# Attention on one core: projections and V spread over the steps, denominators and V in the output's PSUM bank

## The chip, the core and the metric

The kernel runs on one core of a Trainium2 chip. The metric is the device time of one execution in microseconds; the runs of the kernel before took 3674.70, 3674.92 and 3675.24 us (median 3674.92). Five engines share the work, each with a queue of its own that runs in order: TensorE (PE; its weight loads are shown as PEld), VectorE (DVE), ScalarE (ACT), GpSimd (POOL) and SyncE (SP, which issues DMAs). They wait for one another by semaphores.

## The reference, cut to what matters

The program chains four blocks (attention with feed-forward, a residual convolution block, whitening, a state-space block). The change touches attention alone:

```python
x_ln = layer_norm(x_flat, g1, beta1)               # 16 images, 1024 positions, 64 channels
q, k, v = jnp.split(x_ln @ w_qkv.T, 3, axis=-1)    # 8 heads of 32
scores = jnp.einsum('bhqd,bhkd->bhqk', q, k) * HEAD_DIM ** (-0.5)
attn = jax.nn.softmax(scores, axis=-1)
out = jnp.einsum('bhqk,bhkd->bhqd', attn, v)
```

## The kernel before, in words

Layer normalisation has written `scratch_xn`. `attention_phase` (from L144) takes 16 images of 8 heads, in groups of 4 heads (the 128 partitions): 32 groups, one *period* each. A period has 16 steps: 2 halves of 512 queries by 8 blocks of 128 keys (`s`, and `half, kb = divmod(s, 8)`). A lead-in period comes first; the stages are called lead, first, mid and last. Each engine's block has a `period` of its own, an order written out by hand, and the orders meet in counted semaphores.

In a step TensorE makes the scores of 4 heads, transposed (keys on partitions), in fp32 (L398), and adds the negated row maxima to them with a matmul over one row of ones (L402) from `nrow`. ScalarE takes two heads at a time through exp into `probs` (L479). The scores fill one set of four PSUM banks, so a pair of the next step waits until that pair has been read. TensorE then adds the product of V and `probs` of an earlier step into the bank `O` (`values`, L410).

Beside this, for the next group, TensorE makes bf16 scores in the other orientation (`maxima`, L334): four matmuls a step into a ring of three PSUM banks, which VectorE reduces to maxima (L526). After the eight quads of a half VectorE combines them (L534), TensorE turns them (`turn`, L372) and ScalarE copies them to `nrow`. `LATE` says by how many steps the maxima of a group run into its own period. The ring also takes all else: the projections q and k for the next group (`project`, L347), copied by ScalarE to `QT`, `KT` (L461) and cast by VectorE from the same bank to bf16 `QH`, `KH` (L542); V's projection in two banks (`values_projected`, L360); the denominators (`denominators`, L385). `extra` names the step in which each of these stands, and `wait_for_bank` makes TensorE wait until a bank's last reader is done.

A denominator is the sum of `probs` over all keys. GpSimd adds blocks 0 to 5 of a half (L580, five additions into `prob_sums`); a matmul with ones then sums blocks 6 and 7 and `prob_sums`, one step after the half has ended. ScalarE makes exp(-ln) of it (L461, L465), VectorE multiplies `O` by that into `att` (`normalise`, L549), and only then may TensorE start the next half's values in `O`. SP stores `att` and loads the next image's `xn` (L286, L282).

Of the kernel before, what the change touches and what calls it, by code (L numbers as in the profile page):

```python
# [11 lines left out]
P = 128  # L12
# [135 lines left out]
def attention_phase(nc, sem, xn_d, wqkvT, ident_bf, attn_d):  # L148
# [3 lines left out]
    LATE = 3  # L152
# [12 lines left out]
    def executed(stage, kind, which, s):  # L165

        ahead = kind in MADE_AHEAD or (kind == "turn" and which == 0) or (kind == "max" and s >= LATE)
        if stage == "lead":
            return ahead
        if stage == "last":  # L170
            return not ahead
        return not (stage == "first" and kind == "den" and which == 1)
# [45 lines left out]
    with ExitStack() as ctx:  # L218
# [25 lines left out]
                 "negm_done", "sc_ready", "exp_done", "pv_done", "pool_sums", "lden_done", "rden_done", "od_free")  # L244
        (consts_in, consts_set, xn_in, max_ready, max_done, extra_ready, extra_done, cast_done, negm_done, sc_ready,
         exp_done, pv_done, pool_sums, lden_done, rden_done, od_free) = (sem(f"at_{n}") for n in names)
# [12 lines left out]
        def first_groups(grp):  # L259
            return isinstance(grp, int) and grp <= 0  # L260

        def casts(grp, kind, which):
            return 4 * (grp + 1) + 2 * which + "qk".index(kind) + 1
# [11 lines left out]
        def _(sp):  # L275
# [13 lines left out]
            def image(b, stage):  # L289
                if stage != "first":  # L290
                    store(b - 1, 1, 1)
                if stage != "last":

                    at = "first" if stage == "first" else "mid"
                    sp.wait_ge(extra_ready, unit_count(at, GROUPS * b, unit_of(at, "v", 1)))
# [16 lines left out]
        def _(pe):  # L312
# [3 lines left out]
            def wait_for_bank(stage, grp, unit):  # L316
                before = same_bank_before(stage, grp, unit)
                if before:
                    pe.wait_ge(max_done if before[2][1] == "max" else extra_done, unit_count(*before))
                    if before[2][1] in "qk":  # L320

                        pe.wait_ge(cast_done, casts(before[1], *before[2][1:3]))

            def maxima(stage, grp, par, s, heads):
# [4 lines left out]
                if quad == 0 and heads[0] == 0:  # L329
                    pe.wait_ge(cast_done, 4 * (grp + later) + 4)  # L330
# [6 lines left out]
            def project(stage, grp, par, half):  # L337
                if not executed(stage, "q", half, 0):
                    return
                if half == 0 and par == 1:  # L340
                    pe.wait_ge(xn_in, (grp + 3) * DMA)
                units = [unit_of(stage, kind, half) for kind in "qk"]
                for n, unit in enumerate(units):
                    wait_for_bank(stage, grp, unit)
                    rows = slice(n * C, (n + 1) * C)
                    at = n * INNER + (1 - par) * P
                    nc.tensor.matmul(ring[:, unit[3], :], w[rows, at:at + P], xn[rows, hs(half)],  # L347
                                     start=True, stop=True).then_inc(extra_ready, 1)

            def values_projected(stage, grp, par):  # L350
                if not executed(stage, "v", 0, 6):
                    return
                units = [unit_of(stage, "v", n) for n in range(2)]
                for unit in units:
                    wait_for_bank(stage, grp, unit)
                at = 2 * INNER + (1 - par) * P
                for k in range(KB):
                    n = k % 2
                    rows = slice(n * C, (n + 1) * C)
                    m = nc.tensor.matmul(ring[:, units[n][3], blk(k // 2)], xn[rows, blk(k)], w[rows, at:at + P],  # L360
                                         start=True, stop=True)
                    if k >= KB - 2:
                        m.then_inc(extra_ready, 1)
# [12 lines left out]
            def denominators(stage, grp, half):  # L376
                if not executed(stage, "den", half, 0):
                    return
                unit = unit_of(stage, "den", half)
                wait_for_bank(stage, grp, unit)  # L380
                pe.wait_ge(pool_sums, SUMMED * (2 * (grp - half) + half + 1))
                srcs = [probs[:, k, :, :] for k in range(SUMMED + 1, KB)] + [prob_sums[:, half, :, :]]
                for n, src in enumerate(srcs):
                    for h in range(GH):
                        m = nc.tensor.matmul(ring[head(h), unit[3], :], ones[:, head(h)], src[:, h, :],  # L385
                                             start=(n == 0), stop=(n == len(srcs) - 1))
                m.then_inc(extra_ready, 1)

            def scores(stage, grp, par, s):
                half, kb = divmod(s, KB)  # L390
                if kb == 0:

                    at = stage if half else stage_before(stage, grp)
                    pe.wait_ge(extra_done, unit_count(at, grp if half else grp - 1, unit_of(at, "turn", half)))
# [10 lines left out]
            def values(grp, par, s):  # L405
                half, kb = divmod(s, KB)
                if kb == 0 and not (isinstance(grp, int) and grp == 0 and half == 0):
                    pe.wait_ge(od_free, 2 * grp + half)
# [4 lines left out]

            def period(grp, par, stage):
                for s in range(STEPS):
                    if stage != "lead":
                        scores(stage, grp, par, s)
                    maxima(stage, grp, par, s, (0, 1))
                    if s < 2:
                        project(stage, grp, par, s)  # L420
                    if s % KB == 1 and stage != "lead":
                        denominators(stage, grp, 1 - s // KB)
                    if s == 4 or s == 12:
                        turn(stage, grp, 1 if s == 4 else 0)
                    if s == 6:
                        values_projected(stage, grp, par)
                    if stage != "lead":
                        if s == 0:
                            if stage != "first":
                                values(grp - 1, 1 - par, STEPS - 1)  # L430
                        elif s % KB == 2:
                            values(grp, par, s - 2)
                            values(grp, par, s - 1)
                        elif s % KB != 1:
                            values(grp, par, s - 1)
                    maxima(stage, grp, par, s, (2, 3))
                if stage == "last":
                    pe.wait_ge(exp_done, 2 * STEPS * NG)
                    values(grp, par, STEPS - 1)
                    D = ring[:, 0, :]  # L440
                    pe.wait_ge(max_done, counted_before(N_MAX, grp) + N_MAX["last"])
                    pe.wait_ge(extra_done, counted_before(N_EXTRA, grp) + N_EXTRA["last"])
                    pe.wait_ge(pool_sums, SUMMED * 2 * NG)
# [1297 lines left out]
```

## Time and profile before

| | us |
|---|---|
| median of three runs | 3674.92 |
| profiled execution, span | 3666.4 |
| of it, first to last exponential of attention | about 1869 |
| TensorE busy (its matmuls overlap) | 3163.0 |
| VectorE busy | 2573.4 |
| GpSimd busy | 2214.4 |
| ScalarE busy | 2006.1 |

The span is that of one profiled execution, from its first to its last instruction; some 8.5 us of the measured time lie around it. Times below are us from the start of the span. A timeline row gives the start, the time from first start to last end, the engine, the line and operation, the tiles (out<-in), the shapes and the number of instructions merged; in brackets stands the idle time before it and what ended it. In fp32 one matmul of the program is two records. Records of matmuls on different rows or columns of the array overlap, so TensorE's pace is read from starts, not from busy time.

### The profile page before, as it was taken

The numbers are of one execution on the slowest core, as the hardware profiler recorded it, in microseconds if no ns is written. First come the engines' busy times: TensorE is split into PE (matmuls) and PEld (weight loads), VectorE is DVE, ScalarE is ACT, GpSimd is POOL, SyncE is SP. The second block draws the span as 40 slices with busy tenths as digits, with TensorE's granted clock in tenths as the row PEclk, the third lists the DMA queues.
The fourth block names the chain that finished last, engine by engine and source line by source line (L and its number), as shares of the span: only waits on it lengthen the run. The fifth ranks groups of instructions, "written<-read, shape, count | busy, mean of one in ns | idle before, by whom it ended". The sixth has DMA issues, their size and how long they took to land. (4 is left out here: it accounts for less than half of the span.)

```text
span 3666.4 us, 55668 instructions
## 1 busy us (share of the span) xinstructions
PE 3163.0 (86%) x18550; PEld 1183.9 (32%) x18550; DVE 2573.4 (70%) x3346; ACT 2006.1 (55%) x2381; POOL 2214.4 (60%) x684
## 2 busy tenths in 40 slices
PE   6999999999999999999995899774888888887787
PEld 2333333333333333333331233341322222222222
DVE  5777777777767777777771222142888988988988
ACT  3566666666656666666663333223555564565554
POOL 0577777777777777777776000003657666666666
PEclk7899999999999999999998999886989999999999
DMA  2000000000000000000003211114333433443443
GB/s 103 12 16 10 16 16 16 16 13 16 16 17 10 16 16 16 19 10 16 16 10 74 92 69 46 48 64 149 119 132 128 155 142 120 153 150 118 147 150 115
DMA packets 74739, 234.86 MB, mean 64 GB/s; under 512 B 13088, under 2 KB 14180, under 8 KB 74420
## 3 DMA queue, kind: packets, MB, share of 16 engines
q1 hardware_dynamic: 69460, 215.06, 17.3%
q0 software_dynamic: 5056, 16.83, 1.3%
q8 instruction: 139, 2.28, 0.3%
q14 instruction: 84, 0.69, 0.1%
HBM read 192.42 MB, written 39.39 MB: 63 GB/s over the span
## 5 line engine op out<-in xcount | busy, mean ns | idle before, releaser
L526 DVE TENSOR_REDUCE at_pmax<-at_ring 128x1 f32<-128x512 f32 x2048 | 1300.8, 685 | 392.0 <-PE at_ring L334 381.2
L479 ACT ACTIVATE at_probs<-at_sc 128x1024 f32<-128x1024 f32 x1024 | 992.5, 1021 | 531.7 <-PE at_sc L402 529.7
L580 POOL TENSOR_TENSOR at_prob_sums<-at_prob_sums,at_probs 128x2048 f32<-128x2048 f32 x256 | 1159.0, 4527 | 74.8 <-ACT at_probs L479 54.5
L398 PE MATMUL at_sc<-at_QT,at_KT 32*128 32x512 f32 x4096 | 782.5, 634 | 4.1 <-issue 3.7
L1634 POOL TENSOR_TENSOR ss_drive<-ss_du,ss_bsb 128x1024 f32<-128x1024 f32 x261 | 610.7, 2352 | 263.9 <-DVE ss_state L1591 257.1
L1534 ACT ACTIVATE ss_decay<-ss_delta,ss_a 128x512 f32<-128x512 f32 x520 | 354.5, 687 | 447.6 <-DVE ss_state L1587 299.5
L410 PE MATMUL at_O<-at_probs,at_V 128*32 128x512 f32 x4096 | 535.3, 606 | 52.5 <-DVE at_att L549 51.6
L580 POOL TENSOR_TENSOR at_prob_sums<-at_probs 128x2048 f32<-128x2048 f32 x64 | 290.7, 4543 | 403.1 <-ACT at_probs L479 403.1
L1423 PE MATMUL ss_Y<-ss_seen,ss_ident 128*128 128x512 f32 x1032 | 520.7, 628 | 0.0
L334 PE MATMUL at_ring<-at_KH,at_QH 32*128 32x512 bf16 x2048 | 442.3, 387 | 5.7 <-DVE at_pmax L526 2.9
L1599 DVE TENSOR_TENSOR ss_seen<-ss_state,ss_C 128x1024 f32<-128x1024 f32 x259 | 316.3, 1221 | 80.4 <-PE ss_C L1411 72.6
L1591 DVE TENSOR_TENSOR_SCAN ss_state<-ss_decay,ss_state,ss_drive 128x512 f32<-128x512 f32 x259 | 332.3, 1283 | 33.6
L1587 DVE TENSOR_TENSOR_SCAN ss_state<-ss_decay,ss_drive 128x512 f32<-128x512 f32 x259 | 314.9, 1216 | 32.0 <-POOL ss_drive L1634 16.2
L334 PEld LDWEIGHTS at_ring<-at_KH,at_QH 32*128 32x128 bf16 x2048 | 149.6, 92 | 554.5 <-DVE at_pmax L526 345.0
L1411 PE MATMUL ss_C<-ss_bc,ss_select 96*128 96x512 bf16 x518 | 161.0, 393 | 191.5 <-DVE ss_seen L1599 190.9
L402 PE MATMUL at_sc<-at_nrow,at_ones_bf 1*128 1x512 bf16 x2048 | 315.5, 379 | 0.0
L1423 PEld LDWEIGHTS ss_Y<-ss_seen,ss_ident 128*128 128x128 f32 x1032 | 202.3, 200 | 228.7 <-issue 175.5
L398 PEld LDWEIGHTS at_sc<-at_QT,at_KT 32*128 32x128 f32 x4096 | 256.3, 184 | 50.3 <-ACT at_probs L479 40.8
L938 POOL DMA_DIRECT2D scratch_x<-fc_out x8 | 4.3, 534 | 345.9 <-ACT fc_out L839 345.9
L410 PEld LDWEIGHTS at_O<-at_probs,at_V 128*32 128x32 f32 x4096 | 87.4, 108 | 249.3 <-issue 165.9
L1411 PEld LDWEIGHTS ss_C<-ss_bc,ss_select 96*128 96x128 bf16 x518 | 40.4, 101 | 385.8 <-DVE ss_seen L1599 322.7
L347 PE MATMUL at_ring<-at_xn,at_w 64*128 64x512 f32 x256 | 123.7, 679 | 26.6 <-DMA at_xn<-scratch_xn 19.3
(199 smaller groups left out, 2695.6 us busy)
## 6 DMA issues: line engine op xcount, KB each, us to landing
ss_bsb<-scratch_rows SPq DMA_DIRECT2D x265, 512.0 KB, 6.9
scratch_attn<-at_att SPq DMA_DIRECT2D x64, 256.0 KB, 2.0
fc_att<-scratch_attn SPq DMA_DIRECT2D x32, 512.0 KB, 5.8
ss_xn<-scratch_xm SPq DMA_DIRECT2D x34, 256.0 KB, 5.6
at_xn<-scratch_xn SPq DMA_DIRECT2D x32, 256.0 KB, 3.8
ss_xw<-scratch_xw SPq DMA_DIRECT2D x17, 256.0 KB, 3.9
ln_x<-in_x SPq DMA_DIRECT2D x8, 512.0 KB, 4.2
scratch_xn<-ln_xn POOLq DMA_DIRECT2D x8, 512.0 KB, 3.0
```

What stands on the lines that cost most here:

```text
L334: nc.tensor.matmul(ring[:, unit[3], :], QH[head(h), p, blk(quad // 2)], KH[head(h), p, hs(quad % 2)], start=True, stop=True).then_inc(max_ ...
L398: nc.tensor.matmul(sc[:, h, :], KT[head(h), par, blk(kb)], QT[head(h), par, hs(half)], start=True, stop=False)
L402: m = nc.tensor.matmul(sc[:, of, :], ones_bf[row, :], nrow[row, half, :], start=False, stop=True)
L410: m = nc.tensor.matmul(O[head(h), :], V[:, par, kb, head(h)], probs[:, kb, h, :], start=(kb == 0), stop=(kb == KB - 1))
L479: nc.scalar.activation(probs[:, kb, two, :].rearrange("p h q -> p (h q)"), sc[:, two, :].rearrange("p h q -> p (h q)"), ACT.Exp, scale=SCA ...
L526: nc.vector.tensor_reduce(pmax[:, quad // 2, h, quad % 2:quad % 2 + 1], ring[:, unit[3], :], AX_X, ALU.max, negate=True).then_inc(max_done, 1)
L580: nc.gpsimd.tensor_tensor(prob_sums[:, half, :, :], before, probs[:, k, :, :], ALU.add).then_inc(pool_sums, 1)
L1423: m = nc.tensor.matmul(Y[:, hs(h)], ident[:], seen[:, n % DEPTH, hs(h)], start=False, stop=(n == N - 1))
L1534: nc.scalar.activation(decay[:, hs(h)], delta[:, par, hs(h)], ACT.Exp, scale=a_neg[:, n:n + 1])\
L1591: nc.vector.tensor_tensor_scan(now[:, hs(1)], decay[:, hs(1)], drive[:, n % DEPTH, hs(1)], now[:, HALF - 1:HALF], ALU.mult, ALU.add).then_ ...
L1599: nc.vector.tensor_tensor(seen[:, n % DEPTH, :], state[:, n % 2, :], Cp[:], ALU.mult).then_inc(seen_done, 1)
L1634: nc.gpsimd.tensor_tensor(drive[:, n % DEPTH, :], du[:, par, :], bsb[:, n % SLOTS, :], ALU.mult).then_inc(drive_done, 1)
```

## The change

The plan of a period is drawn up anew; no arithmetic goes except two casts' source.

- Projections stand singly: q0 in step 0, k0 in 2, k1 in 3, q1 in 11 (before: q0 and k0 in step 0, q1 and k1 in step 1). Their casts read `QT` and `KT` in SBUF instead of the ring bank, and stand behind the step's reductions.
- V's projection leaves the ring. It is made in two halves, in steps 3 and 11, each of four key blocks in the bank `O`, and copied from there.
- Denominators leave the ring too. When the last values of a half are in `O` (step 0 or 8), ScalarE copies `O` unnormalised to `att`; then TensorE sums blocks 6 and 7 in `O` (step 1 or 9) and adds `prob_sums` (step 2 or 10), and ScalarE takes Ln from `O`. `normalise` multiplies `att` in place, one step later than before.
- `O` is thus used in turn by the values, the denominators and V, with a wait at each change of hands.
- Values are added two blocks at a time: none in steps 1 to 3 of a half, blocks 0 and 1 in its step 4, 2 and 3 in 5, 4 and 5 in 6, 6 in 7, and 7 in the next half's step 0.
- `LATE` goes from 3 to 5; the turns move to steps 7 and 15. The wait for a turn stands between the scores of heads 0 and 1 and their maxima's matmul, not ahead of all scores.

```diff
-    LATE = 3
+    LATE = 5
-    extra = {0: [("q", 0), ("k", 0)], 1: [("q", 1), ("k", 1), ("den", 1)], 4: [("turn", 1)], 6: [("v", 0), ("v", 1)],
-             9: [("den", 0)], 12: [("turn", 0)]}
-    MADE_AHEAD = ("q", "k", "v")
+    extra = {0: [("q", 0)], 2: [("k", 0)], 3: [("k", 1)], 7: [("turn", 1)], 11: [("q", 1)], 15: [("turn", 0)]}
+    MADE_AHEAD = ("q", "k")
+    DIRECT_AT, SUMS_AT, V_AT = 1, 2, 3
+
+    LAST_KB = KB - 1
+    PV_AT = {0: (LAST_KB,), 4: (0, 1), 5: (2, 3), 6: (4, 5), 7: (6,)}
...
                 if before:
                     pe.wait_ge(max_done if before[2][1] == "max" else extra_done, unit_count(*before))
-                    if before[2][1] in "qk":
-
-                        pe.wait_ge(cast_done, casts(before[1], *before[2][1:3]))
...
+            def values_projected(stage, grp, par, half):
+                if stage == "last":
                     return
+                if stage == "lead" or (stage == "first" and half == 0):
+                    if v_halves(grp, half) > 1:
+                        pe.wait_ge(v_done, v_halves(grp, half) - 1)
+                else:
+                    pe.wait_ge(lden_done, 2 * grp + half)
                 at = 2 * INNER + (1 - par) * P
+                rows = slice(half * C, (half + 1) * C)
+                for n in range(KB // 2):
+                    k = half * KB // 2 + n
+                    m = nc.tensor.matmul(O[:, blk(n)], xn[rows, blk(k)], w[rows, at:at + P], start=True, stop=True)
+                m.then_inc(v_ready, 1)
...
+            def denominator(src, start, stop):
+                for h in range(GH):
+                    m = nc.tensor.matmul(O[head(h), :], ones[:, head(h)], src[:, h, :], start=start, stop=stop)
+                return m
+
+            def denominators_direct(of_half):
+                pe.wait_ge(raw_done, of_half + 1)
+                for k in range(SUMMED + 1, KB):
+                    denominator(probs[:, k, :, :], k == SUMMED + 1, False)
+
+            def denominators_sums(of_half, half):
+                pe.wait_ge(pool_sums, SUMMED * (of_half + 1))
+                denominator(prob_sums[:, half, :, :], False, True).then_inc(den_ready, 1)
...
                     nc.tensor.matmul(sc[:, h, :], KT[head(h), par, blk(kb)], QT[head(h), par, hs(half)], start=True, stop=False)
+                    if kb == 0 and h == 1:
+                        at = stage if half else stage_before(stage, grp)
+                        pe.wait_ge(extra_done, unit_count(at, grp if half else grp - 1, unit_of(at, "turn", half)))
...
                     maxima(stage, grp, par, s, (0, 1))
+                    if closes and kb == DIRECT_AT:
+                        denominators_direct(2 * grp + half - 1)
+                    if closes and kb == SUMS_AT:
+                        denominators_sums(2 * grp + half - 1, was_half)
+                    if kb == V_AT:
+                        values_projected(stage, grp, par, half)
                     if stage != "lead":
+                        for k in PV_AT.get(kb, ()):
+                            if kb:
+                                values(stage, grp, par, half, k)
+                            elif closes:
+                                values(stage, was_grp, was_par, was_half, k)
+                    for kind, which in extra.get(s, []):
+                        if kind == "turn":
+                            turn(stage, grp, which)
+                        else:
+                            project(stage, grp, par, kind, which)
                     maxima(stage, grp, par, s, (2, 3))
...
+            def take_raw(grp, half):
+                act.wait_ge(pv_done, STEPS * grp + KB * (half + 1))
+                if not (isinstance(grp, int) and grp == 0):
+                    act.wait_ge(att_stored[half], grp * DMA)
+                nc.scalar.activation(att[:, half, :], O[:], ACT.Copy).then_inc(raw_done, 1)
...
+                nc.scalar.activation(lden[:], O[:], ACT.Ln).then_inc(lden_done, 1)
...
+            def take_v(grp, par, half):
+                act.wait_ge(v_ready, v_halves(grp, half))
+                nc.scalar.activation(V[:, 1 - par, half * KB // 2:(half + 1) * KB // 2, :].rearrange("p k d -> p (k d)"), O[:],
+                                     ACT.Copy).then_inc(v_done, 1)
...
-                    nc.vector.tensor_copy(to[:, 1 - par, hs(which)], ring[:, unit[3], :]).then_inc(cast_done, 1)
+                nc.vector.tensor_copy(to[:, 1 - par, hs(which)], of[:, 1 - par, hs(which)]).then_inc(cast_done, 1)
...
-                nc.vector.tensor_tensor(att[:, half, :], rden[:], O[:], ALU.mult).then_inc(od_free, 1)
+                nc.vector.tensor_tensor(att[:, half, :], att[:, half, :], rden[:], ALU.mult).then_inc(od_free, 1)
```

On ScalarE, `take_raw`, the two steps of the reciprocal, `take_v` and the copies of a step's `extra` stand in this order behind the two exponentials of their step.

## Rows read from the trace of the kernel before

**Rows 1.** Windows: us, then busy us of PE, PEld, DVE, ACT, POOL; clock, DMA.
```profile
1164.90:1223.10 58.20, 55.27 (x468) 21.05 (x465) 44.64 (x73) 37.59 (x45) 45.32 (x11) 1.00 0.06 19
104.90:1974.50 1869.60, 1770.76 (x14728) 669.45 (x14722) 1392.18 (x2246) 1197.55 (x1399) 1446.38 (x320) 0.99 0.05 14
54.50:104.90 50.40, 37.07 (x94) 9.66 (x94) 35.21 (x60) 5.25 (x8) 0.00 (x0) 0.50 0.08 19
```

**Rows 2.** Waits of the period from 1164.9 to 1223.1: total us, times, longest.
```profile
ACT at_probs L479 <- PE at_sc L402: 16.5, 15, 2.3
DVE at_pmax L526 <- PE at_ring L334: 11.6, 13, 2.1
```

**Rows 3.** Timeline of TensorE, steps 7 and 8 of that period.
```profile
1192.84 1.24 PE L398 MATMUL at_sc<-at_QT,at_KT 32*128 32x512 f32 x8
...
1194.03 0.38 PE L334 MATMUL at_ring<-at_KH,at_QH 32*128 32x512 bf16 x2
1194.34 1.06 PE L410 MATMUL at_O<-at_probs,at_V 128*32 128x512 f32 x8
...
1195.34 1.58 PE L398 MATMUL at_sc<-at_QT,at_KT 32*128 32x512 f32 x6
...
1197.49 1.06 PE L410 MATMUL at_O<-at_probs,at_V 128*32 128x512 f32 x8
...
1198.50 1.35 PE L398 MATMUL at_sc<-at_QT,at_KT 32*128 32x512 f32 x8
```

**Rows 4.** Timeline of TensorE, steps 0, 1, 4 and 6 of that period.
```profile
1165.66 2.01 PE L347 MATMUL at_ring<-at_xn,at_w 64*128 64x512 f32 x4
1167.60 1.06 PE L410 MATMUL at_O<-at_probs,at_V 128*32 128x512 f32 x8
...
1172.01 1.92 PE L385 MATMUL at_ring<-at_probs,at_ones 128*32 128x512 f32 x16
...
1174.73 0.39 PE L334 MATMUL at_ring<-at_KH,at_QH 32*128 32x512 bf16 x2
...
1183.63 0.40 PE L372 MATMUL at_ring<-at_ident,at_negm 128*128 128x128 bf16 x4
1183.96 1.06 PE L410 MATMUL at_O<-at_probs,at_V 128*32 128x512 f32 x8
...
1190.75 1.16 PE L360 MATMUL at_ring<-at_w,at_xn 64*128 64x128 f32 x16 [0.82 <-DVE at_pmax L526]
1191.84 1.07 PE L410 MATMUL at_O<-at_probs,at_V 128*32 128x512 f32 x8
```

**Rows 5.** Timeline of ScalarE in that period, with the next one's first exponentials.
```profile
1164.89 1.94 ACT L479 ACTIVATE at_probs<-at_sc 128x1024 f32<-128x1024 f32 x2 [0.56 <-PE at_sc L402]
...
1174.86 0.60 ACT L461 ACTIVATE at_lden<-at_ring 128x512 f32<-128x512 f32 x1 [1.96 <-PE at_ring L385]
...
1176.12 1.94 ACT L479 ACTIVATE at_probs<-at_sc 128x1024 f32<-128x1024 f32 x2
...
1194.23 1.94 ACT L479 ACTIVATE at_probs<-at_sc 128x1024 f32<-128x1024 f32 x2 [1.20 <-PE at_sc L402]
...
1223.07 1.94 ACT L479 ACTIVATE at_probs<-at_sc 128x1024 f32<-128x1024 f32 x2 [0.56 <-PE at_sc L402]
```

**Rows 6.** Groups of instructions, VectorE: shapes, count | busy us, mean ns.
```profile
L542 DVE CAST at_QH<-at_ring 128x512 bf16<-128x512 f32 x64 | 44.3, 692 | 54.1 <-ACT at_QT L461 54.1
...
L900 DVE COPY fc_pad<-fc_pad 64x512 f32<-64x512 f32 x32 | 12.1, 418 | 90.8 <-ACT fc_pad L823 90.8
```

**Rows 7.** The line of the state-space stage's scan: ns min/median/max.
```profile
L1587 DVE TENSOR_TENSOR_SCAN ss_state<-ss_decay,ss_drive x259: 1200/1217/1225, 2553.0 to 3654.9; 128x512 f32<-128x512 f32 x130
```

**Rows 8.** Timeline of the state-space stage: GpSimd's additions.
```profile
2960.49 13.89 POOL L1634 TENSOR_TENSOR ss_drive<-ss_du,ss_bsb 128x1024 f32<-128x1024 f32 x6 [0.25 <-POOL ss_du L1648]
```

**Rows 9.** Timeline of GpSimd in attention: a half's additions, the next half's first.
```profile
1148.37 18.34 POOL L580 TENSOR_TENSOR at_prob_sums<-at_prob_sums,at_probs 128x2048 f32<-128x2048 f32 x4
1172.00 4.54 POOL L580 TENSOR_TENSOR at_prob_sums<-at_probs 128x2048 f32<-128x2048 f32 x1 [5.29 <-ACT at_probs L479]
```

More of the change, by code:

```diff
@@ L169, in executed @@
             return ahead
-        if stage == "last":
-            return not ahead
-        return not (stage == "first" and kind == "den" and which == 1)
+        return not ahead if stage == "last" else True
     def period_units(stage):
@@ L328, in maxima @@
                 p = par if later == 0 else 1 - par
-                if quad == 0 and heads[0] == 0:
-                    pe.wait_ge(cast_done, 4 * (grp + later) + 4)
+                for kind, which, at in (("k", 0, 0), ("k", 1, 1), ("q", 1, KB)):
+                    if quad == at and heads[0] == 0:
+                        pe.wait_ge(cast_done, casts(grp + later - 1, kind, which))
                 for h in heads:
@@ L335, in maxima, with project @@
                                      start=True, stop=True).then_inc(max_ready, 1)
-            def project(stage, grp, par, half):
-                if not executed(stage, "q", half, 0):
+            def project(stage, grp, par, kind, half):
+                if not executed(stage, kind, half, 0):
                     return
-                if half == 0 and par == 1:
+                if (kind, half) == ("q", 0) and par == 1:
                     pe.wait_ge(xn_in, (grp + 3) * DMA)
[L342 to L348, printed above, removed]
@@ L350, in values_projected @@
-            def values_projected(stage, grp, par):
-                if not executed(stage, "v", 0, 6):
-                    return
-                units = [unit_of(stage, "v", n) for n in range(2)]
-                for unit in units:
-                    wait_for_bank(stage, grp, unit)
-                at = 2 * INNER + (1 - par) * P
[L357 to L363, printed above, removed]
+                unit = unit_of(stage, kind, half)
@@ L403, in scores, with values @@
                         m.then_inc(sc_ready, 1)
[L405 to L408, printed above, removed]
+            def values(stage, grp, par, half, kb):
+                if kb == 0:
+                    if stage == "last":
+                        pe.wait_ge(lden_done, 2 * grp + half)
+                    else:
+                        pe.wait_ge(v_done, v_halves(grp, half))
+                if kb == KB - 1:
+                    pe.wait_ge(exp_done, 2 * (STEPS * grp + KB * half + kb) + 2)
                 for h in range(GH):
@@ L412, in values, with half_before @@
                 m.then_inc(pv_done, 1)
+            def half_before(grp, par, half):
+                return (grp, par, 0) if half else (grp - 1, 1 - par, 1)
             def period(grp, par, stage):
                 for s in range(STEPS):
+                    half, kb = divmod(s, KB)
+                    closes = stage != "lead" and not (stage == "first" and half == 0)
+                    was_grp, was_par, was_half = half_before(grp, par, half)
                     if stage != "lead":
@@ L469, in period @@
                     half, kb = divmod(s, KB)
+                    closes = stage != "lead" and not (stage == "first" and half == 0)
                     if stage != "lead":
```

136 lines of the change are left out of this document (51 added, 85 removed).

## Prediction

> **What bounds the kernel now.** I read the stretches of the windows view first, then the waits of one period, then the PE and ACT timelines of that period. Attention has 32 periods of 16 steps, 1870 of the 3666.4 us between its first exponential and its last [rows 1], and nothing outside attention is touched. A regular period, from the first exponential of one group to that of the next, takes 1223.07 - 1164.89 = 58.18 us [rows 5]. In it VectorE is busy 44.6 us, ScalarE 37.6, GpSimd 45.3, and the granted clock is 1.00 (2.4 GHz) [rows 1]: no engine but TensorE is near full, and TensorE's 55 us count overlapping matmuls. ScalarE waits 16.5 us for scores and VectorE 11.6 us for maxima, both from TensorE [rows 2]. So the order of TensorE's queue, and the places where it stands still, set the period.
>
> A plain step shows the unit of work [rows 3]. Scores start at 1192.84 (call it T), the values matmul starts 1.50 us later and takes 1.00 us, and the next scores start at 1195.34: 2.50 us without a gap. The exponentials start at T + 1.39 and the pair ends at T + 3.33 (1194.23 and 1.94 long) [rows 5]. That is 0.83 us after the next scores began; the second pair of heads needs that half of the score banks, so in the next step the values matmul comes 1.32 us after the end of the exponentials (1197.49 against 1196.17) and the step takes 3.16 us. Hence my rule: the work behind the scores starts at T + 1.50 or at E + 1.32, whichever is later, E being the end of the exponentials of the step before. A step in which TensorE has about 0.8 us more to do covers ScalarE for nothing.
>
> **The ledger before.** TensorE's extra pieces, each measured to the start of the next piece [rows 4]: denominators of three sources 1174.73 - 1172.01 = 2.72, so 0.86 for each source after the first, which costs 1.00 as a values matmul does; a V projection 1.09; a turn 0.33; q and k one behind the other 1.94, about 1.0 each when not side by side. A period then holds 16 x 1.50 + 15.7 for the values (two of them in pairs at 1.86) + 5.4 + 2.1 for q and k side by side + 1.1 + 0.7 = 49 us. The other 9 us are waits: for ring banks around the doubled projections (steps 0, 1, 6), for the normalisation before the first values of a half (steps 2, 10), and for exponentials in the short steps (3, 4, 8, 12, 14).
>
> **The change, part by part.** *It adds work to TensorE.* Four single projections cost 4.0 instead of 2.1, and V in two halves 2 x 1.09 instead of 1.09. V's bound: a half uses one row half alone, with as many matmuls in series as now run in each of two streams; if the two streams gain nothing today it is 0.55, so 0.55 to 1.09, and I take 1.09 because the serial pace is what the row shows. Work per period goes from 49 to about 52.
>
> *It takes waits away.* The steps, by the rule above (values pairs 1.86, direct denominators 1.86, sums 1.00):
> - steps 4 to 6 and 12 to 14: 1.50 + 1.86 = 3.36 each. E falls at T + 3.33, just covered.
> - steps 7 and 15: 1.50 + 1.00 + 0.33, plus a little for the ring bank under the turn: 2.90.
> - steps 8 and 0: a new wait. The bias matmul now waits for the turned maxima of the step before, whose copy on ScalarE stands behind its exponentials: T7 + 3.33 + 0.60 = 1.03 us into step 8. Behind it in TensorE's queue stand the scores of heads 2 and 3, and behind them all else. 1.03 + 1.32 + 1.00 = 3.35; step 0 has q0 as well, 4.35.
> - steps 1 and 9: 1.50 + 1.86 = 3.36. The direct denominators wait for the copy of the output, done at about 0.7 us into the step (E plus 0.6) against the 1.50 at which they could start. Cover 0.8.
> - step 10: 1.50 + 1.00 = 2.50; step 2 with k0: 3.50.
> - step 11: E is 0.83 into it, so 2.15, then V and q1, 2.09: 4.24. V waits for the Ln that empties the bank, done 1.4 us into the step. Cover 0.8. Step 12's values wait for the copy of V, which ends about 0.3 us into step 12. Cover 1.2.
> - step 3: ScalarE has exponentials, Ln, Exp (1.26 us until the next exponential could start [rows 5]) and then the copy of k0 from the ring: 3.33 + 1.26 + 0.60 - 3.50 = 1.69 us into step 3. The first maximum behind it uses that ring bank and waits; its place was 1.2 [rows 3]. So 2.0 + 2.09 = 4.09.
>
> Sum: 4.35 + 3.36 + 3.50 + 4.09 + 10.08 + 2.90 = 28.28 for the first half and 3.35 + 3.36 + 2.50 + 4.24 + 10.08 + 2.90 = 26.43 for the second, 54.71 in all: 3.47 us less than 58.18, 6%.
>
> *What is moved on the other engines.* ScalarE gets two copies more (0.6 each), of V the same two: 38.8 us of 54.7. VectorE keeps its reductions; its casts now read SBUF. A cast from PSUM takes 692 ns; a copy of 64 x 512 fp32 between SBUF tiles took 418 [rows 6], so the casts cost between 0.42 and 0.69 and gain nothing on the path. The normalisation reads SBUF twice instead of SBUF and PSUM, 0.69 taken as it is; it comes one step later and TensorE no longer waits for it, and its store leaves one step later, with a period in hand. The loads of the next image move from step 6 to step 11 on SP's queue and have five steps, over 16 us, until step 0 needs them. GpSimd's five additions take 4.54 + 18.34 us [rows 9] and must be done by the sums of step 2 or 10: they start at E of step 1, so end 26.3 us later, some 6 us before they are asked for. With a half of 26.4 us they still fit.
>
> *Ends.* Two of thirteen maxima steps leave the lead-in, which runs at 0.50 of the clock [rows 1] and at VectorE's pace, 44.64 / 73 = 0.61 us each: 8 x 0.61 = 5 us. The last group gains about what a regular one does.
>
> Against the profiled execution: 3666.4 - 32 x 3.47 - 5 = 3550 us of span. The 8.5 us between the span and the median of 3674.92 stay: **3559 us**.
>
> **A rule of the Trainium skill against a row.** In the state-space stage a scan with two SBUF inputs takes 1200 to 1225 ns in all 259 cases [rows 7], while GpSimd's additions run one behind another, six in 13.89 us [rows 8]: neither slows the other. The Trainium skill, page "SBUF — State Buffer", section "Who interferes with whom", says that a VectorE instruction with two SBUF inputs contends with a GpSimd instruction that reads SBUF. By it the new normalisation could stand up to an addition's 4.5 us; by the rows it stands not at all, and the trace disagrees with the rule.
>
> **Rivals.**
> 1. *The casts stand behind GpSimd's additions* (the slower side). No row before shows a fast copy on VectorE beside a GpSimd addition, so its price lies between 0 and one addition, 4.53 us, for each cast. If a cast cannot start until the running addition ends, and VectorE's reductions queue behind it: with an addition every 4.58 us from 3.33 us into step 1, k0's cast is due 8.6 us after T1, inside the second addition (7.9 to 12.5). It waits 3.9 us; the maxima of step 3 find no bank, and the step grows by 3.4. k1's cast meets the next one and costs 1.1, q1's 0.2; q0's falls in GpSimd's idle time. 54.7 + 4.7 = 59.4 us, 1.2 more than now: 3674.9 + 38 - 5 = **3708 us**. It decides against the change as soon as the four casts together hold TensorE for more than 3.5 us in a period. For it: GpSimd is busy 45 of 58 us [rows 1]. Against it: the rows of the scans, which show no such thing for two-input operations. The same section of the Trainium skill says that casts between SBUF tiles may run in a two-port mode, and that the second of the two to issue then blocks fully; no run here shows it yet.
> 2. *The covers are too thin.* The output's bank changes hands between TensorE and ScalarE six times a period, with covers of 0.8 to 1.2 us. If half of these cost a copy of 0.6, the period is 56.5: 32 x 1.7 + 5 = 59 less, **3616 us**. For it: ScalarE takes its work in order, behind the exponentials.
> 3. *The change does nothing for the period*: what TensorE gains as waits it gives back as work (3 us more), **3675 us**. Against it: the waits before add to 9 us.
>
> **How the numbers follow.** Forecast 57%; rival 2 17%; rival 1 17%; rival 3 5%; better than 3515 (TensorE without any wait would need 52 us a period) 4%. The forecast's own range is 3525 to 3595; with the rivals 3515 to 3700, which leaves out the far half of rival 1 and the best case. A difference of 0.2%, 7 us, is what can be told from none. Faster: 57 + 17 + 4, 0.78; same, rival 3, 0.05; slower, rival 1, 0.17.
>
> **What would show it.** Right: exponentials of the same step 54 to 55 us apart; steps 4 to 6 alike at 3.4; step 8 near 3.3 with the second pair of scores behind the turned maxima; TensorE's wait for the normalisation gone. Wrong: casts longer than 0.7 us or late, with reductions queued behind them in steps 3 and 4 (rival 1); TensorE idle ahead of the direct denominators, V or the first values for a ScalarE copy (rival 2).

## The result, and the profile after

The changed kernel takes 4078.15 us (4075.72 to 4079.34) against 3674.92: a ratio of 1.110 [1.108, 1.112]. It is 403 us slower, where 116 us less was forecast, and it lies outside the range. The profiled execution has a span of 4076.5 us.

A regular period, from the first exponential of a group to the next group's, alternates between 70.4 and 72.9 us (even and odd groups); it was 58.18. I measured each step as the time between the starts of its exponentials and the next step's, and took medians over the periods. Twelve of the sixteen steps stand within about a microsecond of the forecast. The rest does not: step 3 takes 8.40 us (forecast 4.09), step 4 takes 9.03 or 10.19 (3.36), step 5 takes 3.35 or 5.41 (3.36), step 12 takes 9.51 or 8.86 (3.36).

The groups of instructions point at VectorE (shapes, count | busy us, mean ns | idle time before and what ended it):

```profile
L503 ACT ACTIVATE at_probs<-at_sc 128x1024 f32<-128x1024 f32 x1024 | 992.0, 1020 | 1048.2 <-PE at_sc L406 1048.2
L338 PE MATMUL at_ring<-at_KH,at_QH 32*128 32x512 bf16 x2048 | 536.6, 417 | 261.2 <-DVE at_pmax L541 260.2
L556 DVE CAST at_KH<-at_KT 128x512 bf16<-128x512 f32 x64 | 275.7, 4308 | 3.5 <-ACT at_KT L466 3.5
L561 DVE TENSOR_TENSOR at_att<-at_att,at_rden 128x512 f32<-128x512 f32 x64 | 233.6, 3649 | 40.7 <-ACT at_rden L483 40.7
```

A cast that was to cost 0.42 to 0.69 us takes 4.3 on the mean, and the normalisation, taken at 0.69, takes 3.6. TensorE waits 261 us ahead of its maxima matmuls, nearly all of it for VectorE's reductions; before the change it was 5.7 us:

```profile
L334 PE MATMUL at_ring<-at_KH,at_QH 32*128 32x512 bf16 x2048 | 442.3, 387 | 5.7 <-DVE at_pmax L526 2.9
```

What VectorE's instructions last, one line of the kernel at a time (min/median/max in ns), shows that a cast is not slow as such: those of q take 0.42 as often as not, those of k nearly never:

```profile
L556 DVE CAST at_QH<-at_QT x64: 416/424/3547, 62.9 to 2309.1; 128x512 bf16<-128x512 f32 x64
L556 DVE CAST at_KH<-at_KT x64: 427/4342/4765, 65.6 to 2276.5; 128x512 bf16<-128x512 f32 x64
L561 DVE TENSOR_TENSOR at_att<-at_att,at_rden x64: 692/3771/3790, 144.1 to 2388.7; 128x512 f32<-128x512 f32 x64
```

Beside GpSimd's additions it becomes plain when they are slow. The timeline of one odd period (from 1465.0 to 1537.9 us) for VectorE, without the reductions between the lines (start, time from start to end):

```profile
1469.43 0.42 DVE L556 CAST at_QH<-at_QT 128x512 bf16<-128x512 f32 x1
...
1476.33 4.27 DVE L556 CAST at_KH<-at_KT 128x512 bf16<-128x512 f32 x1
...
1481.72 3.79 DVE L561 TENSOR_TENSOR at_att<-at_att,at_rden 128x512 f32<-128x512 f32 x1
...
1486.63 4.76 DVE L556 CAST at_KH<-at_KT 128x512 bf16<-128x512 f32 x1
...
1517.65 3.71 DVE L561 TENSOR_TENSOR at_att<-at_att,at_rden 128x512 f32<-128x512 f32 x1
...
1522.48 3.54 DVE L556 CAST at_QH<-at_QT 128x512 bf16<-128x512 f32 x1
```

And for GpSimd in the same period (compare [rows 9]):

```profile
1471.20 4.53 POOL L593 TENSOR_TENSOR at_prob_sums<-at_probs 128x2048 f32<-128x2048 f32 x1 [9.38 <-ACT at_probs L503]
1475.81 9.15 POOL L593 TENSOR_TENSOR at_prob_sums<-at_prob_sums,at_probs 128x2048 f32<-128x2048 f32 x2
1486.59 4.52 POOL L593 TENSOR_TENSOR at_prob_sums<-at_prob_sums,at_probs 128x2048 f32<-128x2048 f32 x1 [1.63 <-ACT at_probs L503]
```

The first cast, at 1469.43, meets no addition and takes 0.42 us. The cast at 1476.33 starts 0.52 us into an addition; that one, half of 9.15 long, ends near 1480.4, and the cast ends at 1480.60. The normalisation at 1481.72 starts inside the next addition, which ends at 1484.96, and ends at 1485.51. The cast at 1486.63 starts 0.04 us behind an addition that ends at 1491.11, and ends at 1491.39. Every slow one ends 0.2 to 0.6 us behind an addition, somewhat less than it takes by itself. Over the whole trace there is no exception: of 128 casts and 64 normalisations 155 start while an addition runs, and each of them ends 0.28 us (casts) or 0.55 us (normalisations) behind that addition; the other 37 take 0.42 to 0.43 or 0.69. Between 1476.33 and 1491.39 VectorE spends 12.8 us in three instructions that together need 1.5.

TensorE's timeline shows what that does (in brackets the idle time and its releaser), beside a pair of values of a step that is not disturbed in the kernel both_moved (below), where it takes 1.92:

```profile
1481.26 0.39 PE L338 MATMUL at_ring<-at_KH,at_QH 32*128 32x512 bf16 x1 [3.02 <-DVE at_pmax L541]
...
1486.17 0.60 PE L338 MATMUL at_ring<-at_KH,at_QH 32*128 32x512 bf16 x1 [1.30 <-DVE at_pmax L541]
1486.70 3.64 PE L418 MATMUL at_O<-at_probs,at_V 128*32 128x512 f32 x16
```

```profile
1466.80 1.92 PE L418 MATMUL at_O<-at_probs,at_V 128*32 128x512 f32 x16
```

The reductions stand behind the cast in VectorE's queue, so no ring bank comes free; TensorE's maxima matmul waits, and with it the scores that stand behind it in TensorE's queue. ScalarE then has nothing to exponentiate. The first wait, 3.02 us, is the larger part of what step 3 loses (8.40 us against 3.47 in both_moved). Then, in step 4, the pair of values takes 3.64 us instead of 1.92. The windows of that period say why (us, busy time and number for PE, PEld, DVE, ACT, POOL, then the granted clock):

```profile
1465.00:1476.00 11.00, 11.00 (x90) 3.74 (x86) 7.52 (x14) 8.44 (x11) 4.72 (x2) 1.00 0.01 1
1476.00:1485.00 9.00, 5.63 (x31) 2.41 (x27) 9.00 (x5) 3.52 (x6) 8.88 (x2) 0.82 0.00 1
1485.00:1495.00 10.00, 7.67 (x34) 2.00 (x34) 9.01 (x9) 1.75 (x3) 4.52 (x1) 0.50 0.07 26
```

After the stall the granted clock stands at 0.50 (1.2 GHz), and what TensorE has to do there takes nearly twice as long. Before the change the clock stood at 1.00 over a whole period [rows 1]. So there are two losses, one behind the other: the waits, and TensorE's work at half clock behind them.

### The profile page after: what moved, and what is told of

Read it like the earlier page. It is cut to its first block and busy times, and to the rows that moved or that the text cites. A ratio compares the mean times of both kernels' runs of the same rounds, so it can differ in the third digit from the quotient of the medians.

```text
span 4076.5 us, 55661 instructions
## 1 busy us (share of the span) xinstructions
PE 3416.4 (84%) x18550; PEld 1229.9 (30%) x18550; DVE 3049.3 (75%) x3346; ACT 2029.6 (50%) x2445; POOL 2225.7 (55%) x684
## 5 line engine op out<-in xcount | busy, mean ns | idle before, releaser
L593 POOL TENSOR_TENSOR at_prob_sums<-at_prob_sums,at_probs 128x2048 f32<-128x2048 f32 x256 | 1171.2, 4575 | 227.4 <-ACT at_probs L503 211.8
L338 PE MATMUL at_ring<-at_KH,at_QH 32*128 32x512 bf16 x2048 | 536.6, 417 | 261.2 <-DVE at_pmax L541 260.2
L418 PE MATMUL at_O<-at_probs,at_V 128*32 128x512 f32 x4096 | 635.6, 737 | 0.8 <-ACT at_probs L503 0.8
L406 PE MATMUL at_sc<-at_nrow,at_ones_bf 1*128 1x512 bf16 x2048 | 300.8, 402 | 0.1
L556 DVE CAST at_KH<-at_KT 128x512 bf16<-128x512 f32 x64 | 275.7, 4308 | 3.5 <-ACT at_KT L466 3.5
L561 DVE TENSOR_TENSOR at_att<-at_att,at_rden 128x512 f32<-128x512 f32 x64 | 233.6, 3649 | 40.7 <-ACT at_rden L483 40.7
L418 PEld LDWEIGHTS at_O<-at_probs,at_V 128*32 128x32 f32 x4096 | 114.1, 123 | 293.0 <-issue 291.3
```

Of the source, the lines that this page charges most:

```text
L338: nc.tensor.matmul(ring[:, unit[3], :], QH[head(h), p, blk(quad // 2)], KH[head(h), p, hs(quad % 2)], start=True, stop=True).then_inc(max_ ...
L418: m = nc.tensor.matmul(O[head(h), :], V[:, par, kb, head(h)], probs[:, kb, h, :], start=(kb == 0), stop=(kb == KB - 1))
L593: nc.gpsimd.tensor_tensor(prob_sums[:, half, :, :], before, probs[:, k, :, :], ALU.add).then_inc(pool_sums, 1)
```

## The experiments

**Theory A**: a VectorE instruction that reads two inputs from SBUF, or casts between SBUF tiles, cannot run while a GpSimd instruction runs that reads SBUF; it waits for that one's end, and all that is queued behind it waits too. **Theory B**: the schedule is at fault (too much work on TensorE, or bank `O` passed from hand to hand too late), and the long instructions are only its companions. Later **theory C**: only GpSimd's large additions in attention do this. That came from the rows of the state-space scans [rows 7, 8], which seemed to speak against A.

| kernel | casts | normalisation | period, us | time, us |
|---|---|---|---|---|
| before | VectorE, from PSUM | VectorE, one input in PSUM | 58.18 | 3674.92 |
| after | VectorE, from SBUF | VectorE, both in SBUF | 70.4 / 72.9 | 4078.15 |
| norm_pool | as after | GpSimd | 56.66 | 3639.61 |
| cast_act | ScalarE | as after | 61.96 (about every third 60.4) | 3771.00 |
| norm_scan | ScalarE | VectorE, a scan, both in SBUF | 61.4 | 3774.41 |
| split_adds | ScalarE | as after, additions in halves | 54.7 | 3553.76 |
| both_moved | ScalarE | GpSimd | 53.64 | 3524.41 |
| short_adds | as after | as after, additions a quarter as large (three heads left out) | 53.64 | 3518.47 |
| before_sbuf_casts | VectorE, from SBUF | as before | 61.5 | 3771.03 |

The period is the median of the profiled execution. All but both_moved (and the change itself) are single timings; the kernel before took 3663.9 to 3677.4 beside them, so differences of 100 us and more are far outside the spread.

**both_moved.** The plan of the change stays; neither kind of instruction is left on VectorE. ScalarE casts behind the exponentials of steps 1, 4, 5 and 12, and GpSimd normalises behind its first addition of a half.

```diff
+                    for kind, which in {1: [("q", 0)], 4: [("k", 0)], 5: [("k", 1)], 12: [("q", 1)]}.get(s, []):
...
+                            nc.scalar.activation(to[:, 1 - par, hs(which)], of[:, 1 - par, hs(which)], ACT.Copy).then_inc(cast_done, 1)
...
-                    if s == 3 and stage not in ("lead", "first"):
-                        normalise(grp - 1, 1)
-                    if s == KB + 3 and stage != "lead":
-                        normalise(grp, 0)
...
-                    for kind, which in extra.get(s, []):
-                        if kind in MADE_AHEAD:
-                            cast(stage, grp, par, kind, which)
...
+                nc.gpsimd.tensor_tensor(att[:, half, :], att[:, half, :], rden[:], ALU.mult).then_inc(od_free, 1)
...
+                        if k == 1 and half == 1:
+                            normalise(grp, 0)
+                        if k == 1 and half == 0 and stage != "first":
+                            normalise(grp - 1, 1)
...
```

> The changed kernel with the two VectorE steps that now read only SBUF taken off VectorE: the four casts on ScalarE, behind the exponentials of steps 1, 4, 5 and 12, and the normalisation on GpSimd, behind the first addition of a half. All sums are kept. Theory A (such a VectorE instruction cannot start while a GpSimd addition runs; the reductions queue behind it, TensorE finds no ring bank, and its clock falls to half): nothing is left that waits, a period comes to the 54.7 us of the prediction, about 3560 us in all, granted clock 1.00 in attention. Theory B (the new order itself loses the time: late casts, hand-overs of the output's bank, the wait for the turned maxima): the period stays above 65 us, over 3900 us.

It took 3524.41 us, 0.961 [0.959, 0.964] of the kernel before, which took 3665.93 beside it. It is faster than both kernels of this case. The window of one period (columns as above) shows TensorE busy over all of it and the clock at 1.00:

```profile
1456.30:1509.95 53.65, 53.65 (x468) 20.65 (x464) 40.49 (x67) 40.37 (x51) 47.78 (x12) 1.00 0.03 11
```

The steps, by exponentials, are 4.23, 3.35, 3.55, 3.47, 3.36, 3.36, 3.35, 3.05 and 3.18, 3.36, 3.00, 3.27, 3.36, 3.35, 3.35, 3.07 (medians); the period is 53.64 us. Theory B has fallen: the schedule is good, better than I had it.

**cast_act and norm_pool.** Each makes one half of that diff only. cast_act:

```diff
+                            nc.scalar.activation(to[:, 1 - par, hs(which)], of[:, 1 - par, hs(which)], ACT.Copy).then_inc(cast_done, 1)
...
-                            cast(stage, grp, par, kind, which)
```

norm_pool:

```diff
-                    if s == 3 and stage not in ("lead", "first"):
-                        normalise(grp - 1, 1)
-                    if s == KB + 3 and stage != "lead":
-                        normalise(grp, 0)
...
+                nc.gpsimd.tensor_tensor(att[:, half, :], att[:, half, :], rden[:], ALU.mult).then_inc(od_free, 1)
```

> The changed kernel with the four casts on ScalarE (behind the exponentials of steps 1, 4, 5 and 12); the normalisation stays on VectorE with both inputs in SBUF. Theory A: the casts' part of the loss goes, the normalisations still take about 3.7 us each and hold the reductions of steps 3 and 11; some 2 us of a stall each and a spell of half clock, period about 60 us, some 3725 us. Theory B: about as the changed kernel, 4078 us.

> The changed kernel with the normalisation on GpSimd, behind the first addition of a half; the casts stay on VectorE and read SBUF. Theory A: casts of k0, k1 and q1 still take 3 to 5 us, period 64 to 66 us, some 3850 us. Theory B: about as the changed kernel, 4078 us.

Durations on the lines of the normalisation in cast_act and of the casts in norm_pool:

```profile
L566 DVE TENSOR_TENSOR at_att<-at_att,at_rden x64: 693/3412/3777, 145.6 to 2081.4; 128x512 f32<-128x512 f32 x64
```

```profile
L556 DVE CAST at_QH<-at_QT x64: 415/423/2787, 63.8 to 1872.1; 128x512 bf16<-128x512 f32 x64
L556 DVE CAST at_KH<-at_KT x64: 426/1614/3183, 66.5 to 1844.8; 128x512 bf16<-128x512 f32 x64
```

Normalisations alone cost 61.96 - 53.64 = 8.3 us a period by the medians, casts alone 3.0; by the means of all periods it is 7.8 and 3.6. Together, in the change, they cost 18 (71.7 on the mean less 53.64), so the two are not additive. The clock differs too: from 300 to 900 us the granted clock is 1.00 in both_moved, 0.99 in norm_pool, 0.95 in cast_act and 0.87 in the change. Both sizes were missed: cast_act came out 46 us above what was expected, norm_pool some 200 below. Without the normalisations in VectorE's queue the casts start elsewhere in an addition, and wait 1.2 us instead of 3.9. How long such an instruction waits is set by where in an addition it happens to start.

**short_adds.** GpSimd's additions are cut instead, to the first head, 512 of 2048 columns; the sums of the other three heads are a constant that VectorE writes once at the start.

```diff
-nc.gpsimd.tensor_tensor(prob_sums[:, half, :, :], before, probs[:, k, :, :], ALU.add).then_inc(pool_sums, 1)
+nc.gpsimd.tensor_tensor(prob_sums[:, half, 0:1, :], before[:, 0:1, :], probs[:, k, 0:1, :], ALU.add).then_inc(pool_sums, 1)
```

> The changed kernel with GpSimd's additions cut to the first head, 512 of 2048 columns; the denominators of the other three heads lack blocks 0 to 5, a constant stands in their place. All waits and VectorE steps are as in the changed kernel. Theory A: a VectorE step waits for one addition of some 1.2 us at most, so casts take at most 1.7 us and the normalisation at most 2, period 55 to 57 us, about 3600 us. Theory B: 4078 us.

```profile
L557 DVE CAST at_QH<-at_QT x64: 415/417/426, 63.4 to 1760.5; 128x512 bf16<-128x512 f32 x64
L557 DVE CAST at_KH<-at_KT x64: 415/416/427, 66.1 to 1734.5; 128x512 bf16<-128x512 f32 x64
L562 DVE TENSOR_TENSOR at_att<-at_att,at_rden x64: 677/680/693, 144.3 to 1830.3; 128x512 f32<-128x512 f32 x64
```

With VectorE's and TensorE's work in the periods untouched, all long instructions are gone, and the period is that of both_moved to the hundredth. The additions (now 1.3 us) were the cause. It is faster than theory A had it, since hardly one of these instructions meets an addition any more: none of the 128 casts, and one of the 64 normalisations, starts while one runs.

**before_sbuf_casts.** The other side: the kernel before, in which only the source of the casts is changed.

```diff
-nc.vector.tensor_copy(to[:, 1 - par, hs(which)], ring[:, unit[3], :]).then_inc(cast_done, 1)
+nc.vector.tensor_copy(to[:, 1 - par, hs(which)], of[:, 1 - par, hs(which)]).then_inc(cast_done, 1)
```

> The kernel before with one part of the change alone: the four casts read the copies in SBUF instead of the ring bank. Theory A: the casts of step 0 fall in GpSimd's idle time and take 0.42 us; of those in step 1 the first meets the first addition of the half and takes about 4.5 us, TensorE waits for the bank behind it, and a period grows by 3 to 4 us: about 3780 us. Theory B: casts of 0.42 us instead of 0.69, no more than 3675 us.

```profile
L542 DVE CAST at_QH<-at_QT x64: 426/429/4382, 63.5 to 1968.5; 128x512 bf16<-128x512 f32 x64
L542 DVE CAST at_KH<-at_KT x64: 411/426/428, 64.0 to 1972.9; 128x512 bf16<-128x512 f32 x64
```

Only one cast a period, q1's in step 1, falls into an addition. It takes 4.38 us instead of 0.69 [rows 6], step 1 goes from 6.13 to about 9.3, and the kernel is 107 us slower than the one before beside it. One operand's place, in the old schedule, was enough.

**norm_scan.** cast_act with the normalisation replaced by a scan, the form of [rows 7], of the same size, with both inputs in SBUF.

```diff
-nc.vector.tensor_tensor(att[:, half, :], att[:, half, :], rden[:], ALU.mult).then_inc(od_free, 1)
+nc.vector.tensor_tensor_scan(att[:, half, :], rden[:], att[:, half, :], 0.0, ALU.mult, ALU.add).then_inc(od_free, 1)
```

> As the kernel with the casts on ScalarE, but the normalisation on VectorE is a scan over the same two SBUF tiles (state = rden * state + unnormalised output), which is not the quotient: the output of attention is left wrong. It asks why the state-space stage's scans beside GpSimd misled the prediction. Theory A1 (a scan with two SBUF inputs does not wait for GpSimd, an elementwise product does): the scan takes about 1.22 us, the period is 55 to 56 us, some 3590 us. Theory A2 (both wait; in the state-space stage something else keeps them apart): the scan takes 3 to 5 us here, some 3750 us.

```profile
L566 DVE TENSOR_TENSOR_SCAN at_att<-at_rden,at_att x64: 1225/3943/4316, 145.6 to 2082.0; 128x512 f32<-128x512 f32 x64
```

The scan waits as the multiplication does. So [rows 7] could not mean what I had read in them. The code says why: `ss_decay` is allocated as a PSUM tile. Each of those scans reads SBUF once. The next run tests that reading.

**before_decay_sbuf.** The kernel before, with `ss_decay` in SBUF and nothing else changed.

```diff
-aux, decay, Cp, Y = ps("ss_aux"), ps("ss_decay"), ps("ss_C"), ps("ss_Y")
+decay = sb("ss_decay", [P, S])
+aux, Cp, Y = ps("ss_aux"), ps("ss_C"), ps("ss_Y")
```

> The kernel before, with one tile moved: `ss_decay`, which ScalarE's Exp writes and the state-space scans read, lies in SBUF instead of PSUM. The rows of the scans (1200 to 1225 ns beside GpSimd's additions) were read in the prediction as two-input SBUF operations; but `ss_decay` is a PSUM tile, so each scan there reads SBUF once. Theory A (a VectorE instruction with two SBUF inputs cannot run while a GpSimd operation with SBUF inputs does): now the scan of the first half, which starts 1.1 us after GpSimd's 2.36 us multiplication, waits for that one's end: 1.2 + 1.2 = about 2.4 us and up to 3.6; the step of 3.80 us grows by about 1.2, and some 250 steps by 300 us: 3900 to 4000. Theory C (the state-space stage's GpSimd operations, of 1024 columns, or its scans are of a kind that does not contend): scans stay at 1.20 to 1.23 and the time within 0.5% of the kernel before.

```profile
L1588 DVE TENSOR_TENSOR_SCAN ss_state<-ss_decay,ss_drive x259: 1200/2333/3342, 2552.6 to 3934.0; 128x512 f32<-128x512 f32 x130
```

The time goes to 3946.83 from 3667.25, as A has it: over both lines of the scan, 518 in all, the mean goes from 1.25 to 1.86 us, 316 us in sum, and the kernel takes 280 more. A regular step of the timeline, GpSimd above, VectorE below:

```profile
3115.24 2.35 POOL L1635 TENSOR_TENSOR ss_drive<-ss_du,ss_bsb 128x1024 f32<-128x1024 f32 x1 [2.58 <-DVE ss_state L1592]
```

```profile
3115.20 1.22 DVE L1600 TENSOR_TENSOR ss_seen<-ss_state,ss_C 128x1024 f32<-128x1024 f32 x1
3116.34 2.34 DVE L1588 TENSOR_TENSOR_SCAN ss_state<-ss_decay,ss_drive 128x512 f32<-128x512 f32 x1
3118.81 1.28 DVE L1592 TENSOR_TENSOR_SCAN ss_state<-ss_decay,ss_state,ss_drive 128x512 f32<-128x512 f32 x1
```

`ss_seen`, whose second input `ss_C` is still a PSUM tile, takes 1.22 us, and the multiplication, which starts 0.04 us behind it, 2.35: neither waits for the other. The scan behind it has both in SBUF and takes 2.34: it ends 1.09 us after the multiplication does. C has fallen: GpSimd operations of 1024 columns in the state-space stage do the same.

**split_adds.** cast_act with each addition made as two of 1024 columns.

```diff
-nc.gpsimd.tensor_tensor(prob_sums[:, half, :, :], before, probs[:, k, :, :], ALU.add).then_inc(pool_sums, 1)
+nc.gpsimd.tensor_tensor(prob_sums[:, half, 0:2, :], before[:, 0:2, :], probs[:, k, 0:2, :], ALU.add)
+nc.gpsimd.tensor_tensor(prob_sums[:, half, 2:4, :], before[:, 2:4, :], probs[:, k, 2:4, :], ALU.add).then_inc(pool_sums, 1)
```

> As cast_act (casts on ScalarE, normalisation on VectorE), with each GpSimd addition of 2048 columns made as two of 1024, about 2.3 us each. Nothing is left out. If the wait ends with each GpSimd instruction, the normalisation takes at most 0.69 + 2.3 = 3.0 us, and on the mean about 1.9 instead of 3.3; steps 4 and 12 shrink from 7 or 8 us to about 5, the period from 61.9 to about 57, the time to about 3620. If VectorE gets in only where GpSimd stands still for a semaphore, and not between two instructions that follow each other at once, it stays above 3 us and the time near 3770. If operations of 1024 columns do not contend (theory C), the normalisation takes 0.69 us and the time is near 3530.

One half's normalisation, and the additions around it (VectorE, then GpSimd):

```profile
1462.94 1.70 DVE L566 TENSOR_TENSOR at_att<-at_att,at_rden 128x512 f32<-128x512 f32 x1
```

```profile
1461.72 2.36 POOL L595 TENSOR_TENSOR at_prob_sums<-at_prob_sums,at_probs 128x1024 f32<-128x1024 f32 x1
1464.04 2.82 POOL L596 TENSOR_TENSOR at_prob_sums<-at_prob_sums,at_probs 128x1024 f32<-128x1024 f32 x1
1466.93 2.36 POOL L595 TENSOR_TENSOR at_prob_sums<-at_prob_sums,at_probs 128x1024 f32<-128x1024 f32 x1
```

The normalisation starts 1.22 us into a part, whose end is at 1464.08, and ends at 1464.64. The next part, issued at 1464.04, takes 2.82 us instead of 2.36: now GpSimd waits. So the wait ends with each GpSimd instruction, even when the next follows at once, and whichever instruction comes second waits. The median went from 3.41 to 1.39 us, the time from 3771 to 3553.76. That is lower than the 3620 expected, since a wait of about 1 us costs little of a step: step 4 takes 3.5 us and step 12 takes 4.27, against 3.36. That the maxima's ring absorbs the rest is my reading; no run tests it.

## Why the prediction was wrong, point by point

- **What bounds the kernel, and the rule for a step** held. TensorE's order sets the period: with the long instructions out of the way its records fill the period, 53.65 of 53.65 us.
- **The schedule's sum** held: 54.71 forecast, 53.64 measured in both_moved and short_adds. The rule counts a step from the start of its scores to that of the next, so it is compared that way here. Steps 1, 4 to 6, 9, 10 and 12 to 14 are right to 0.01 us, step 2 to 0.05, steps 0, 7, 8 and 15 to 0.2. Steps 11 (4.24, measured 3.77) and 3 (4.09, measured 3.47) were put too high, and the timeline of both_moved shows the term. A half of V and a single projection were summed as 1.09 + 1.00, but they overlap (V's half is on one half of the rows, the projection on the other), and both together take 1491.21 - 1489.60 = 1.61 us:

```profile
1489.60 0.82 PE L366 MATMUL at_O<-at_w,at_xn 64*128 64x128 f32 x5
1490.16 0.69 PE L351 MATMUL at_ring<-at_xn,at_w 64*128 64x512 f32 x1
1490.26 0.49 PE L366 MATMUL at_O<-at_w,at_xn 64*128 64x128 f32 x3
1490.69 0.59 PE L351 MATMUL at_ring<-at_xn,at_w 64*128 64x512 f32 x1
1491.21 0.39 PE L338 MATMUL at_ring<-at_KH,at_QH 32*128 32x512 bf16 x2
```

- **The ledger before** has a term without a row, 2.1 us for the two pairs of q and k. The pair of [rows 4] took 1.94 and the one in step 1, by the same timeline, 1.65: 3.6 in all. The work before was then some 50.5 us and the waits some 7.7, not 9. The sum of the steps does not use it.
- **Rival 2, thin covers around `O`**, did not come: in the period of both_moved shown above none of TensorE's waits ahead of its work in `O` is for a ScalarE copy. **Rival 3** is out as well: the same schedule without the long instructions takes 0.961 of the time before.
- **"The normalisation reads SBUF twice, 0.69 taken as it is"** is the step that failed. Its own 0.69 us held (0.692 where no addition runs), but its wait was put at nothing. With the wait it took 3.6 us on the mean, the reductions queued behind it, and alone, in cast_act, that cost about 8 us a period. The casts' wait, nothing in the forecast too, cost 3.0 to 3.6 alone, and both together made the period 71.7 us instead of 54.7. The price came from [rows 7, 8], read as a scan with two SBUF inputs beside GpSimd. The line shows only the tiles' names, and `ss_decay` lies in PSUM. With it moved to SBUF the same row reads 2333 ns instead of 1217. No row of the trace before showed two SBUF inputs on VectorE beside GpSimd's arithmetic, so the cost had to be bounded by an addition, 4.53 us, as I did for the casts. With that bound the normalisation would have been a rival with a price and a chance; it had neither.
- **"The trace disagrees with the rule"** falls with it. The Trainium skill, page "SBUF — State Buffer", section "Who interferes with whom", says that a VectorE instruction with at most one SBUF input, outside the two-port modes, does not contend with GpSimd, that one with two SBUF inputs contends with a GpSimd instruction that reads SBUF, and that the port they share is an exclusive lock, with issue order deciding who blocks. By that rule [rows 7] had to be as they are. The traces agree with all three: 1.22 us for `ss_seen`, 3.41 for the normalisation in cast_act, 2.82 for GpSimd's part in split_adds. The casts, on which the prediction had a second sentence from that section of the Trainium skill, wait in the same way (4.3 us on k's lines); in which mode they run, no trace shows.
- **Rival 1** named the right mechanism, with a chance of 17%, but for the casts alone, and so with too small a price: 3708 us against 4078. It had the casts at 4.7 us a period; alone they cost 3.0 to 3.6. In the period shown each waiting instruction delays the next one into another addition, and VectorE's reductions stand behind all of them: 4.27 + 3.79 + 4.76 + 3.71 + 3.54 + 0.42 = 20.5 us there, for six instructions that need 3.1 (2 x 0.69 + 4 x 0.42).
- **What no part of the prediction had** is the clock. Behind the stalls the granted clock is 0.50, and in odd periods step 5 takes 5.41 us instead of 3.35 although VectorE's long instructions are over by then; its own pair of values, at half clock, accounts for 3.64 - 1.92 = 1.7 of the 2.1 us:

```profile
1495.00 3.64 PE L418 MATMUL at_O<-at_probs,at_V 128*32 128x512 f32 x16
```

  The clock was not tested by itself, so how the 18 us divide into waits and half clock is not shown. Why it reaches into step 5 only in every second period stays open.

## What to carry to other kernels

Before an operand is moved from PSUM to SBUF, list the VectorE instructions that then read SBUF twice or cast from SBUF to SBUF, and the GpSimd instructions that run at that time: each may wait for a whole one, and the queue behind it waits too. What helped here was one operand in PSUM, another engine (ScalarE for casts, GpSimd itself for the multiplication), or shorter GpSimd instructions. And when a row of the trace is to price another instruction, look up in the code in which memory each of its tiles lies; the row names tiles, not memories.

## What the runs showed of the hardware

- The wait goes both ways and from instruction to instruction. A normalisation that waited ended about 0.55 us behind the GpSimd instruction it had met; the GpSimd instruction that came next took 2.82 us instead of 2.36 (split_adds).
- GpSimd needed 1.27 us for the normalisation that VectorE does in 0.69 undisturbed, and in both_moved that lengthens nothing: the period is that of short_adds, where VectorE does it.

```profile
1462.89 1.27 POOL L585 TENSOR_TENSOR at_att<-at_att,at_rden 128x512 f32<-128x512 f32 x1
```

- A multiplication with one input in PSUM is as fast as one with both in SBUF and no neighbour: a median of 0.689 us before, where 63 of the 64 start while one of GpSimd's additions runs, against 0.680 in short_adds. Nor did the casts from PSUM wait: 62 of 128 start beside an addition there, and none takes more than 0.69. The place of the operand shows in the time only where GpSimd runs.

```profile
L549 DVE TENSOR_TENSOR at_att<-at_rden,at_O x64: 678/689/689, 147.8 to 1983.9; 128x512 f32<-128x512 f32 x64
```
